# A gated unit in plain fp32 in place of two-part fp32r products, in a four-layer cross-attention kernel

## The reference

```python
def _tlin(x, w, s):
    return jnp.einsum('bsi,oi->bso', x, w) * s
h = jax.nn.silu(_tlin(x, w1_w, w1_s)) * _tlin(x, w2_w, w2_s)
h = jax.nn.gelu(_tlin(h, h1_w, h1_s), approximate=False)
h = jax.nn.gelu(_tlin(h, h2_w, h2_s), approximate=False)
return _tlin(h, w3_w, w3_s)
```

## Time and profile before

| | |
|---|---|
| three timed executions | 1055.20, 1058.17, 1059.38 us; median 1058.17 |
| profiled execution | span 1052.7 us from its first to its last instruction; a time of its own beside the three is not given |
| busy share | PE 92%, PE's weight loads 55%, DVE 74%, ACT 46%, POOL 28% |
| granted clock of PE | mean 0.969 of full speed |
| expert stage | PE from 413 to 499 us |
| gated unit | PE from 736.1 to 907.7 us |
| traffic | 121.81 MB, 116 GB/s over the span |

### The profile page before, as it was taken

One profiled execution on the slowest core, in us unless ns is written; L12 is line 12 of the kernel. 1 busy time (PEld: TensorE's weight loads), 2 busy tenths in 40 slices (PEclk: granted clock), 3 DMA queues, 4 the chain that ended last, 5 costly groups with the idle time before them and its releaser, 6 DMA issues.

```text
span 1052.7 us, 17430 instructions
## 1 busy us (share of the span) xinstructions
PE 971.8 (92%) x6530; PEld 574.6 (55%) x6530; DVE 774.0 (74%) x1445; ACT 488.9 (46%) x708; POOL 290.5 (28%) x439
## 2 busy tenths in 40 slices
PE   8897987999999977999689999999999999899998
PEld 4333353444444454999254444445788788644446
DVE  4989888999999631454489899995664645699956
ACT  2672331477777721121027777776312212347763
POOL 3656710133343203002302433322500400013230
PEclk9998989999999977999899999999999999999999
DMA  6889912103320323995341233201254242110001
GB/s 205 271 266 311 361 35 69 43 25 115 124 86 23 98 85 115 327 374 186 90 150 47 63 84 83 62 9 42 87 192 141 84 140 100 28 45 13 8 2 40
DMA packets 79181, 121.81 MB, mean 116 GB/s; under 512 B 9733, under 2 KB 52904, under 8 KB 79090
## 3 DMA queue, kind: packets, MB, share of 16 engines
q1 hardware_dynamic: 59278, 79.29, 24.3%
q10 hardware_dynamic: 19044, 39.22, 10.7%
q0 software_dynamic: 768, 2.10, 0.6%
HBM read 92.10 MB, written 27.81 MB: 114 GB/s over the span
## 4 chain that ended last, share of the span: by engine, by line
PE 67%; DVE 20%; DMA 5%; issue 3%; ACT 2%; POOL 2%; SPq 0%; DVEq 0%; ACTq 0%; POOLq 0%
PE bank L1601 15%; PE bank L1567 15%; PE bank L1822 12%; DVE arena L2343 10%; PE st_bank L1752 4%; PE bank L1764 4%; DMA kparts<-arena 3%; PE st_bank L1586 3%; PE st_bank L1822 2%; PE bank L1361 2%; PE st_bank L1515 1%; PE bank L1655 1%; PE bank L1620 1%; DVE bnst L1925 1%; PE st_bank L1891 1%
## 5 line engine op out<-in xcount | busy, mean ns | idle before, releaser
L2343 DVE TENSOR_REDUCE arena<-bank 128x1 f32<-128x512 f32 x640 | 397.1, 681 | 33.7 <-PE bank L1567 32.8
L1208 ACT ACTIVATE arena<-st_bank 128x1024 f32<-128x1024 f32 x320 | 312.3, 1022 | 137.1 <-PE st_bank L1586 136.0
L1567 PE MATMUL bank<-g_a 64*128 64x512 f32 x480 | 181.5, 477 | 11.7 <-DVE arena L2343 3.3
L1601 PE MATMUL bank<-arena,vaug 128*9 128x256 f32 (+2 forms) x2560 | 168.5, 381 | 1.3 <-ACT arena L1208 1.3
L1567 PEld LDWEIGHTS bank<-g_a 64*128 64x128 f32 x480 | 73.2, 183 | 124.9 <-DVE arena L2343 100.3
L1822 PE MATMUL bank<-g_a,g_w 128*128 128x512 f32 x512 | 117.3, 390 | 1.1 <-POOL g_a L959 1.1
L1586 PE MATMUL st_bank<-g_a 64*128 64x512 f32 x480 | 115.3, 417 | 0.0
L1822 PEld LDWEIGHTS bank<-g_a,g_w 128*128 128x128 f32 x512 | 95.9, 188 | 21.9 <-POOL g_a L959 2.0
L926 POOL COPY arena<-arena 8x32 f32<-8x32 f32 x160 | 34.8, 217 | 259.4 <-issue 137.2
L1601 PEld LDWEIGHTS bank<-arena,vaug 128*9 128x9 f32 (+2 forms) x2560 | 55.8, 92 | 75.2 <-issue 39.7
L1567 PE MATMUL bank<-g_x,g_a 64*128 64x512 f32 x160 | 63.4, 494 | 9.6 <-DVE arena L2343 3.5
(11 more groups left out here) (329 smaller groups left out, 1442.3 us busy)
## 6 DMA issues: line engine op xcount, KB each, us to landing
arena<-in_glu_w SPq DMA_DIRECT2D x39, 512.0 KB, 3.2
arena<-kv_table SPq DMA_DIRECT2D x11, 1024.0 KB, 7.6
ctxT<-in_glu_w ACTq DMA_DIRECT2D x22, 512.0 KB, 5.9
arena<-in_w SPq DMA_DIRECT2D x20, 512.0 KB, 5.9
kparts<-arena ACTq DMA_DIRECT2D x12, 512.0 KB, 5.4
arena<-in_w ACTq DMA_DIRECT2D x12, 512.0 KB, 3.4
xnT<-kv_table SPq DMA_DIRECT2D x5, 1024.0 KB, 8.0
g_a<-kparts SPq DMA_DIRECT2D x24, 192.0 KB
```

The source lines that it names most:

```text
L1208: act.activation(prob[sl % PROBS], st_bank[sl % 2][:], ACT.Exp, scale=scale).then_inc(exp_ready, 1)
L1567: pe.matmul(bank[TURN_BANKS[place % 3]], Qc[gi % KQ_BUFS][rows, qt * P:(qt + 1) * P], Kc[gi % KQ_BUFS][rows, half * CH:(half + 1) * CH], s ...
L1601: ins = pe.matmul(bank[7][at:at + dh + 1, 0:D], vaug[l][:, b * KT + 2 * m + i, h0 + hh, :], tiles[:, a], start=(m == 0 and i == 0), stop=( ...
L2343: dve.tensor_reduce(mxh[gi % 2][:, col, hf:hf + 1], bank[TURN_BANKS[place % 3]], AX.X, ALU.max).then_inc(max_red, 1)
```

## The change

The unit's buffers become plain fp32. Each product is written once, with the weight straight from the slot that the load filled and the values as ACT or DVE wrote them. The weight slots go from three to eight (four semaphores, one for each pair), ACT loads the first eight and the last layer's two chunks in attention 2, and the last layer's weights stay for both halves. The scan, the flags and the second copy of the unit go, and PE waits for `units_done` in their place. ACT writes Gelu's result and DVE the gated product straight to the hidden buffers; POOL's low parts go. Attention 3's keys and queries get buffers that the unit doesn't use: POOL fills them when attention 2's scores are done, and SP loads all four groups of keys before the unit's remaining chunks. The diff, cut to its core:

```diff
             pass
-        g_x = [sb(f"g_x{i}", [P, DC, T], F32R) for i in range(2)]
-        scan_buf = [ctxT[:, i // 2, i % 2 * GC:(i % 2 + 1) * GC] for i in range(GLU_RAW)]
-        scan_bits = ctxT[:, 1, GC:2 * GC].bitcast(I32)
+        first_keys = sb("first_keys", [P, M], F32R)
+        ctxT_rest = sb("ctxT_rest", [P, DC * CT - M])
...
-        Kc = [g_x[0][:, 0, :]] + [g_a[1][0][:, 2 * i:2 * i + 2, :].rearrange("p a b -> p (a b)") for i in range(KQ_BUFS - 1)]
-        Qc = [g_a[1][0][:, NF - 2, :], g_a[1][0][:, NF - 1, :], g_a[1][1][:, 0, :], g_a[1][1][:, 1, :]]
+
+
+        Kc = [first_keys[:, :]] + [keys_queries[:, i * M:(i + 1) * M] for i in range(KQ_BUFS - 1)]
+        Qc = [keys_queries[:, (KQ_BUFS - 1) * M + i * CH:(KQ_BUFS - 1) * M + (i + 1) * CH] for i in range(KQ_BUFS)]
...
-        r = Region(GLU_WORDS)
-        assert r.at >= after_att
-        g_raw = [r.take([GC]) for _ in range(GLU_RAW)]
+        r = Region(after_att)
+        g_w = [r.take([GC]) for _ in range(GLU_SLOTS)]
+        g_w3 = r.take([NF, D])
...
+                rows3 = slice(part * W3_EACH, (part + 1) * W3_EACH)
+                eng.dma_start(g_w3[:, rows3], io["glu_w"][HALF_CHUNKS + part].rearrange("p (f d) -> p f d", d=D)).then_inc(glu_last, 16)
 
         def glu_chunk_load(eng, n):
-            eng.dma_start(g_raw[n % GLU_RAW], io["glu_w"][GLU_ORDER[n]]).then_inc(glu_raw[n % GLU_RAW], 16)
+            eng.dma_start(g_w[n % GLU_SLOTS], io["glu_w"][n % HALF_CHUNKS]).then_inc(glu_w[n // 2 % len(glu_w)], 16)
...
             def glu_loads():
-                for n in range(GLU_RAW, len(GLU_ORDER)):
-                    sp.wait_ge(glu_split, n - GLU_RAW + 1)
+                for n in range(GLU_SLOTS, 2 * HALF_CHUNKS):
+                    sp.wait_ge(glu_mm, glu_blocks(n - GLU_SLOTS))
                     glu_chunk_load(sp, n)
...
             attention_loads(2)
+            keys_stored(3)
+            for g in range(KQ_BUFS):
+                keys_load(3, g)
             glu_loads()
...
 
-                    for h in range(2):
-                        for f in range(NF):
-                            pool.wait_ge(gated_high, h * NF + f + 1)
-                            pool.tensor_tensor(g_a[0][1][:, f, :], g_tmp[f % 2], g_a[0][0][:, f, :].bitcast(F32), ALU.subtract).then_inc(act_split, 1)
-                    pool.wait_ge(glu_mm, BLOCKS + NF)
+                    pool.wait_ge(st_mm, KT * GROUP0[3])
                     keys_minus_ones(3, 0).then_inc(kq_clear, 1)
+                    for g in range(KQ_BUFS):
+                        if g:
+                            keys_minus_ones(3, g)
+                        queries_zero(3, g)
                 if l == 1:
...
                     keys_minus_ones(2, 0).then_inc(kq_clear, 1)
...
+                            if l == 2 and i < GLU_FIRST:
...
 
-            def scan_loads(first, last):
-
-                for n in range(first, min(last, GLU_CHUNKS)):
-                    if n >= GLU_RAW:
-                        act.wait_ge(scan_done, n - GLU_RAW + 1)
-                    act.dma_start(scan_buf[n % GLU_RAW], io["glu_w"][n]).then_inc(glu_raw[n % GLU_RAW], 16)
-
-            scan_loads(0, 1)
             for e in range(E_MOE):
                 hidden(e, unit_up, unit_hid, unit_down)
...
                 if layer == 0:
-                    ins = act.activation(g_silu[a % 2], bank[f % 2], ACT.Silu, scale=gsc[:, 0, f:f + 1])
+                    n = h * NF + f
+                    if n >= 2:
+                        act.wait_ge(gated, n - 1)
+                    act.activation(g_silu[f % 2], bank[f % 2], ACT.Silu, scale=gsc[:, 0, f:f + 1]).then_inc(glu_silu, 1)
                 else:
-                    ins = act.activation(g_tmp[a % 2], bank[4 + f % 2], ACT.Gelu, scale=gsc[:, 1 + layer, f:f + 1])
-                ins.then_inc(glu_act, 1)
+                    act.activation(g_a[layer % 2][:, f, :], bank[4 + f % 2], ACT.Gelu, scale=gsc[:, 1 + layer, f:f + 1]).then_inc(glu_act, 1)
 
             query_part(3, 0)
-            act.wait_ge(kq_clear, cleared(3, 0) - 1)
-            for g in range(KQ_BUFS):
-                if g:
-                    act.activation(Kc[g], bc(onesf[:, 0:1], [P, M]), ACT.Copy, scale=-1.0)
-                act.activation(Qc[g], bc(zero_row[:, 0:1], [P, CH]), ACT.Copy).then_inc(kq_clear, 1)
-                if g == 0:
-                    first_rests(3)
+            first_rests(3)
             attention(3)
 
...
-            pe.wait_ge(sum_ready, 4)
-            pe.matmul(bank[6][0:1, 0:1], onesf[:, 0:1], low_sum, start=True, stop=True).then_inc(sum_mm, 1)
-            pe.wait_ge(flag_ready, 3)
-
+            pe.wait_ge(units_done, 1)
             hold_clock(LN_HOLDS[4], 2)
             pe.wait_ge(gathered[0], 16 * QT)
             hold_clock(GATHERED_HOLDS, 2)
             attention(2)
 
...
-                    pairs = [(0, 0), (0, 1)] + [(1, 0)] * low_weights
-                    for i, (a, b) in enumerate(pairs):
-                        stationary, moving = (weights[a], tokens[b]) if weights_stay else (tokens[b], weights[a])
-                        ins = pe.matmul(out, stationary, moving, start=(first and i == 0), stop=(last and i == len(pairs) - 1))
...
-                                    at = (j * DC + k) * UP_FS * P + i * P
-                                    ins = split_products(bank[2 * j + f % 2], [v[:, at:at + P] for v in wbuf], [v[:, k, h * CH:(h + 1) * CH] for v in g_x], True,
-                                                         k == 0, k == DC - 1)
...
+                tokens = xnT[:, :, h * CH:(h + 1) * CH]
+                for f in range(NF):
+                    n, c = h * NF + f, h * HALF_CHUNKS + f // UP_FS
+                    if f == 0:
+                        pe.wait_ge(xnT_ready, LN_AT[5] * 4 + DC * (h + 1))
+                    if f % UP_FS == 0:
+                        pe.wait_ge(glu_w[c // 2 % len(glu_w)], 32 * (c // GLU_SLOTS + 1))
+                    if (h, f) == (0, SECOND_TOKENS_AT):
+                        ln_transposes(5, [1], SECOND_BANKS)
+                    if n >= 2:
+                        pe.wait_ge(gated, n - 1)
+                    for j in range(2):
+                        for k in range(DC):
+                            at = ((j * DC + k) * UP_FS + f % UP_FS) * P
+                            ins = pe.matmul(bank[2 * j + f % 2], g_w[c % GLU_SLOTS][:, at:at + P], tokens[:, k], start=(k == 0), stop=(k == DC - 1))
+                    ins.then_inc(glu_mm, 1)
+                if h == 0:
+                    pe.wait_ge(xnT_ready, (LN_AT[5] + 1) * 4)
+                for layer in (1, 2):
+                    src, ready, had = (g_a[0], gated, h * NF) if layer == 1 else (g_a[1], glu_act, 2 * h * NF)
+                    for f in range(NF):
+                        n, c = (2 * h + layer - 1) * NF + f, h * HALF_CHUNKS + UP_CHUNKS + (layer - 1) * NF + f
+                        pe.wait_ge(glu_w[c // 2 % len(glu_w)], 32 * (c // GLU_SLOTS + 1))
                         if (h, layer, f) == (1, 2, TOKENS_AT):
                             ln_transposes(6, [0])
-                        a = h * BLOCKS + layer * NF + f
-                        src = g_a[(layer - 1) % 2]
-                        pe.wait_ge(glu_act, a - 1)
+                        if n >= 2:
+                            pe.wait_ge(glu_act, n - 1)
                         for j in range(NF):
                             if f == 0:
-                                pe.wait_ge(act_split, a - NF + j + 1)
-                            ins = split_products(bank[4 + f % 2], [v[:, j * P:(j + 1) * P] for v in wbuf], [v[:, j, :] for v in src], True, j == 0, j == NF - 1)
+                                pe.wait_ge(ready, had + j + 1)
+                            ins = pe.matmul(bank[4 + f % 2], g_w[c % GLU_SLOTS][:, j * P:(j + 1) * P], src[:, j, :], start=(j == 0), stop=(j == NF - 1))
                         ins.then_inc(glu_mm, 1)
-                        if (h, layer, f) == (1, 2, NF - 1):
-                            query_product(3, 0)
-                    if c == len(GLU_HALF) - 1:
-                        if h == 0:
-                            pe.wait_ge(glu_split, GLU_ORDER.index(W3_FIRST + W3_CHUNKS - 1) + 1)
-                        for q in range(QT):
-                            t = h * QT + q
-                            if t >= 2:
-                                pe.wait_ge(x_ready, 5 * NT + t - 1)
-                            for j in range(NF):
-                                if q == 0:
-                                    pe.wait_ge(act_split, (h + 1) * BLOCKS - NF + j + 1)
-                                ins = split_products(bank[6 + t % 2][:, 0:D], [v[:, j, :] for v in g_w3], [v[:, j, q * P:(q + 1) * P] for v in g_a[0]], False, j == 0, j == NF - 1)
-                            ins.then_inc(out_mm, 1)
-
-            low, no_low = (pe.value_load(low_flags[0:1, i:i + 1], min_val=0, max_val=1) for i in range(2))
...
-                gated_unit(False)
```

(99 more changed lines are left out.)

120 lines of the change are left out of this document (8 added, 112 removed).

## The result

The changed kernel takes 1188.24 us (median; 1185.67 to 1191.74) against 1058.01 for the kernel before: ratio 1.1256, 95% interval 1.1225 to 1.1286. The forecast was 1192.5 in a range from 1184 to 1208. The profiled execution of after took 1187.01, its span is 1185.3.

What follows compares the result with a forecast made beforehand. PE, busy 168.4 of the gated unit's 171.6 us, was taken as the bound. Products +140.5 and waits -6.2 gave +134.3, taking the span from 1052.7 to 1187.0; with 5.5 kept, 1192.5 us, range 1184 to 1208.

Steps and rivals of the forecast that it cites:

- (a): PE's products in the gated unit: 302.1 us as plain fp32 against 161.6 now, +140.5 us, all on the path.
- Rival 1: Gated unit: a plain product costs one record's time, not two, so the change wins; 1041 us, chance 0.02.
- rival 2: Gated unit: each plain record costs what two fp32r products do, 0.456 and 0.246 us; 1213.7 us, chance 0.09.
- rival 4: Gated unit: plain records cost L1909's 0.4425 us each, 8.6 us more; 1201 us, chance 0.15.
- (b): Gated unit: splits by DVE and POOL go, and PE's waits for them with them, -6.2 us.
- cheap products: Gated unit, in (b): were PE's products much cheaper, ACT and DVE would set the pace and the waits would stay.
- (c): Expert stage and its exit: removing the weight scan, its sum and flags gains 0, bounds 0 and -5 us.
- (d): Before the last attention: PE's 1.18 us idle gap gains 0, since DVE holds PE's third product; bound -1.
- Rival 3: Expert stage exit shortens by up to 5 us, the last store landing sooner without scan traffic; 1187.5 us, chance 0.10.
- (e, f): Last attention's keys and queries, POOL fills and SP loads: 0; ACT's seven more loads in attention 2: 0, at most +3.
- the 5.5 us: Whole kernel: difference between the profiled span, 1052.7, and the timed executions' median, kept and added to 1187.0 for 1192.5.

Runs made afterwards that it cites:

- a_half: The changed kernel with four of eight products in each hidden block, half the hidden-width sum left out; 1078.16 us, ratio 1.0215 to the kernel before.
- b_early: The kernel before with PE and ACT released at DVE's multiplication instead of its cast in first-projection blocks; 1052.43 us, ratio 0.9967.
- b_one: The kernel before with only the high x high fp32r product of each pair, DVE and POOL still computing low parts; 1010.59 us, ratio 0.956.
- b_nobranch: The kernel before with scan, sum and flags kept but the branch on PE and DVE removed; 1054.05 us, ratio 1.0005.
- b_noscan: The kernel before without weight scan, flags and second copy of the unit, PE waiting for units_done; 1050.97 us, ratio 0.9961.
- a_keyslate: The changed kernel with SP's key loads for the last attention put back behind the unit's weight loads; 1186.21 us, ratio 1.1241 to the kernel before.
- a_slots4: The changed kernel with four weight slots in place of eight; 1189.43 us, ratio 1.1283 to the kernel before.
- a_slots2: The changed kernel with two weight slots in place of eight; 1309.11 us, ratio 1.2395 to the kernel before.

## Why the prediction was right, and where it was off

**The products (a).** The step that carries the sum. Forecast +140.5 us from spacings of 0.429 and 0.215, read at L1378 and L1899 of the kernel before. Measured in the unit: 0.429, and for the last layers of its two halves 0.216 and 0.219 (13.81 / 64 and 14.03 / 64). The price goes with the columns: the 256-wide records have the same 128 x 128 stationary side and take half as long. a_half shows the price by leaving products out, 109.9 / 128 = 0.858 for one. Rival 1 (one record's time for a product) and rival 2 (0.456 a record) fall with it, and so does rival 4, with 0.4425: over the 640 wide records it would be 8.6 us more.

**The waits (b).** Forecast -6.2: PE becomes the late one. Right: no wait in the unit, busy 306.40 of 306.40 us, and the stage came out at 306.3 for 305.9. b_early shows that 2.5 of the 6.2 were the wait for L2627. b_one shows what was said of cheap products, that the casts would then set the pace, and how hard: of 80.8 us of products 36 are not given back, some 4 of them by the granted clock and nearly 2 by a longer gap behind the unit. The kernel came out 6 us above its expectation.

**Scan (c) and branch (d).** Taken at 0, with bounds of -5 and -1. In the profile of after the two stretches are 94.3 for 94.4 and 144.4 for 143.9: nothing gained in the place that was named, and the 1.2 us of the branch's gap given back to DVE's clearing of the bank, which had been named as the next wait. The branch is shown by b_nobranch to be worth nothing that can be measured. For the scan 0 was too little in the kernel before: b_noscan gains 4.1 us, within the bound that was kept, and by a way that I can't name. Rival 3, that the exit of the expert stage shortens by up to 5, is not it: the exit stayed. Whether the changed kernel has the gain too can't be read: it lies 130.2 us above its before, a_keyslate 131.1 and a_slots4 135.3 above theirs.

**Keys, queries and loads (e, f).** Taken at 0. a_keyslate shows it for the order of the keys, a_slots4 for the loads: even with a chunk asked for 13.7 us ahead of its use instead of 41 nothing waits. The seven more loads on ACT's queue weren't tried alone; the stretch in which they are issued, from the gathers to the unit, is 230.3 for 230.1 us.

**The term that was mis-sized** is the last one, the 5.5 us that "lie between that span and their median". It was taken as if it were one fixed cost. In every execution for which both are known, 124 of them and of all kernels, the time is 1.7 to 1.8 us above the execution's own span. The other 3.7 was spread: the profiled execution of before was a short one (1052.7 + 1.75 = 1054.5, with the batch's own median at 1058.2). So 1.75 belongs on the span, and the spread on the range, not on the value. With a span of 1187.0 this gives 1188.8, against 1188.24 measured; that it comes so near is in part luck, with four executions from 1185.67 to 1191.74. The span itself was forecast 1.7 too long, 1187.0 for 1185.3. Of that 1.3 arose before the expert stage, ahead of all that was forecast: the transposes of L1349 stood at 381.10 and stand, as L1310, at 379.76, well within the 7.6 us over which this point scatters in the twelve profiles. From there to the end the profile grew from 671.6 to 805.5, +133.9, for the +134.3 of the sum.

## What to carry to other kernels

Where PE bounds a stage, price a change of number format by the spacing of its records in the timeline at the same shape, elsewhere in the same kernel if need be, and not by their mean duration (390 and 592 ns here, for 228 and 429 of wall time) or by the count of instructions in the source. A split into two fp32r products costs 0.456 us per 512 columns and one into three 0.68, a plain fp32 product 0.858; the splitting that other engines do is free only as long as PE's products cover it, so before taking it away ask whether it is on the path at all.

## What was not expected of the hardware

A wait of 3.5 us for a load cost PE another 2.9 us afterwards: the granted clock was 0.53 over the 6.1 us that followed and 1.00 behind them, although PE had been busy without a break for 16.8 us before the next such wait, and the next piece was as slow again (16.85 us for 32 records, a_slots2). So in this stage of dense products the short waits for data cost 1.8 times their length (116.9 us for 64.8), and the part above the waits shows neither as idle time nor in the list of waits, only in the clock and in records that stand farther apart. The wait of 3.61 us ahead of 1135.12 cost nothing of the kind, so the drop can't be counted on for each wait.

The surplus of a record over its bare columns goes with the format. A plain record takes 0.429 us for 512 columns, 2.4 ns over two columns' clock each (512 x 2 / 2.4 = 426.7). An fp32r product takes 0.228 and 0.123 us, 14 to 16 ns over 213.3 and 106.7, the same for both widths. That the same kernel shows both side by side, at one clock, is why a spacing couldn't be carried over from the one to the other.
